# Transposing the copied rows instead of a second product of the second mixing: a transformer layer with a router, one core

## The chip, the core and the metric

The kernel runs on one core of a Trainium2 chip. Time is device time in microseconds (us) of one launch; the median of several launches is compared. TensorE is PE in the profile (PEld for its weight loads), VectorE DVE, ScalarE ACT, GpSimd POOL, and the queue that issues most DMAs SP.

## What is computed

128 sequences of 32 tokens with 256 channels (4096 tokens). `x = x + attention(mix1(x))`, then `x = x + experts(mix2(x))`. A mixing multiplies each sequence by a 32 x 32 matrix of its own; the change touches how the second one is done and how its result reaches the router.

```python
w = weights[conditions]                          # one 32 x 32 matrix per sequence
h = jnp.einsum('bct,bcd->bdt', x, w)             # the second mixing
...
scores = jnp.einsum('btd,de->bte', h, router_w)  # 16 experts
probs = jax.nn.softmax(scores, axis=-1)
routing_weights, routing_idx = jax.lax.top_k(probs, K)      # K = 2
...
out = jnp.einsum('ebtd,bte->btd', expert_out, combine)
```

## The kernel before

The tokens are 32 tiles of 128 rows, in 8 groups (`g`) of 4 tiles. A first phase takes every group through first mixing, quantised projections, attention, output projection, second mixing, router and placement: each row of the second mixing is scattered to DRAM (`routed`) at a place in the list of each of its two experts. A second phase goes through 79 tiles of those lists, a third adds the two results per token and writes the output. The change lies in the first phase alone.

The first phase is a software pipeline written out by hand: each engine has an `iteration(it)` that lists its steps, and runs it for `it` = 0 to 11 (below: **pass** 0 to 11). In pass `it` four groups are in work: `it` (first mixing, projections: PE L1104, L1113, L1137, L1142, L1174), `it - 1` (scores L1189 and L1193, soft maximum, `attend` for tiles 0 and 1), `it - 2` (`attend` L1221 for tiles 2 and 3, output projection L1232), `it - 3` (second mixing and router) and `it - 4` (scatter, POOL L502). So pass 8 is the first with no new group, pass 9 has no scores, and pass 10 has group 7's second mixing alone. Each engine takes its list strictly in order, and engines meet through semaphores.

The second mixing of a group is computed twice on TensorE. `mix2_T` (L1257) gives it transposed, channels on partitions, into the banks `ps_h` (`ps_h[0]` is bank `ps_c`, `ps_h[1]` is `ps_a`): 8 products of 128 columns for two tiles at a time. ScalarE copies it to `hT` (`copy_hT`, L686), from which `router` (L1270) takes its operand. `mix2` (L1244) gives the same numbers by rows into `ps_a`, and ScalarE copies them to `hrow` twice, once for each of a token's experts (`copy_h`, L678). An f32 product shows as two records in the trace, a transpose as one.

What follows the router on VectorE: `rivals` (L917, L919: the two largest scores), `route` (L926 to L932, ends in `both`), then in this order `largest_o` (L845), `row_max` of the second score tile (L880), `factor_o` (L851, L853), `scale_k` (L870), `choose` and `place` (L939 to L962), `row_max` of the third tile, `scale_k`, `step_o` (L860), `norm_o` (L889, L891) and `row_max` of the fourth. `factor_o` lets ScalarE's `round_o` (L593) and with it TensorE's transpose L1127 go; `scale_k` lets TensorE's second `project_k` (L1142) go; each `row_max` lets POOL's `sub_max` (L491) go. On POOL the first two tiles' scatters of a group (four L502) follow the fourth `sub_max` of the pass before. TensorE's `rank` (L1283 to L1286) waits for `both` and for `copy_h`, since it writes `ps_a`. On the SP queue `load_bd2` brings the 32 x 32 matrices of a later group, after `hT_ready` and `h_ready` of the group two before it.

The order of the steps on TensorE from the second mixing on:

```python
mix1(it, 0); mix2_T(it - 3, 0); mix1(it, 1)
attend(it - 2, 2); transpose_p(it - 2, 3); mix2_T(it - 3, 1); attend(it - 2, 3)
mix2(it - 3, 0); scores(it - 1, 0); router(it - 3); scores(it - 1, 1)
mix2(it - 3, 1); scores(it - 1, 2); transpose_x(it, 0); transpose_x(it, 1); spread_s(it)
```

## Time and profile before

| | |
|---|---|
| median of 3 runs | 494.92 us (494.81 to 497.31) |
| the profiled execution | 493.43 us, its span 491.7 us |
| first phase | to about 297 us of the span |
| TensorE busy, whole span | 341.8 us (70%) |
| VectorE / ScalarE / POOL busy | 261.6 / 245.1 / 236.3 us |
| mean granted TensorE clock | 0.876 |
| ScalarE: L678, L686 | 32 of 601 ns, 16 of 595 ns |

Times of a row are from the start of the span. "idle before" is the time for which the engine stood still before that row, and the arrow names who ended it. Matmuls overlap, so the length of a piece of TensorE's work is best taken from the start of its row to the start of the next row.

### The profile page before, as it was taken

The page shows a single profiled execution, that of the slowest core. Times are in us where ns is not written, and L with a number is a line of the kernel's source. Part 1 is how long each engine was busy: PE and PEld are TensorE (multiplying, and loading weights), DVE is VectorE, ACT ScalarE, POOL GpSimd, SP SyncE. Part 2 cuts the span into 40 slices and gives each one's busy share as a digit, 9 for nine tenths or more (in the row PEclk, how much of TensorE's full clock was granted, in tenths as well). Part 3 has the DMA queues.
Part 4 walks back from the last instruction along what each step waited for, and adds up shares of the span by engine and source line. Part 5 has one row for each costly group of instructions (what it writes and reads, how often), then busy time and mean ns, then how long its engine had stood idle before and what let it go on. Part 6 is the DMA issues. An engine that isn't in the chain of part 4 may idle for free.

```text
span 491.7 us, 11060 instructions
## 1 busy us (share of the span) xinstructions
PE 341.8 (70%) x3257; PEld 255.5 (52%) x3257; DVE 261.6 (53%) x913; ACT 245.1 (50%) x580; POOL 236.3 (48%) x248
## 2 busy tenths in 40 slices
PE   0456989989989897958755407988789888981000
PEld 0342647666756566645544306777677767760000
DVE  1635587978869797955744462333233423331531
ACT  9152778866869585845642303454444444440000
POOL 3651231246445555463556361555455555555672
PEclk9977999998999999998965657999899989997555
DMA  6506465365362715353557265544354434413994
GB/s 218 142 3 158 64 154 135 57 131 135 78 185 50 206 44 146 80 144 72 142 147 204 92 245 141 157 128 142 108 149 140 149 119 137 143 33 144 326 381 173
DMA packets 76897, 68.87 MB, mean 140 GB/s; under 512 B 41003, under 2 KB 65968, under 8 KB 76721
## 3 DMA queue, kind: packets, MB, share of 16 engines
q1 hardware_dynamic: 65200, 44.03, 36.0%
q0 software_dynamic: 7296, 20.02, 11.2%
q10 hardware_dynamic: 4352, 4.20, 2.5%
q8 instruction: 28, 0.46, 0.4%
q14 instruction: 21, 0.16, 0.1%
HBM read 35.36 MB, written 30.62 MB: 134 GB/s over the span
## 4 chain that ended last, share of the span: by engine, by line
PE 45%; DVE 17%; issue 9%; DMA 6%; another core or an unknown queue 5%; POOL 5%; ACT 5%; DVEq 4%; SPq 1%; POOLq 0%; ACTq 0%
PE bank L1355 12%; PE bank L1366 7%; DMA arena<-y_d 4%; PE bank L1348 3%; PE bank L1193 3%; PE bank L1244 2%; PE bank L1270 2%; PE bank L1221 2%; PE bank L1127 2%; PE bank L1142 2%; POOL arena L549 2%; DVE stats L898 2%; PE bank L1232 2%; DVE amax L851 2%
## 5 line engine op out<-in xcount | busy, mean ns | idle before, releaser
L542 POOL DMA_INDIRECT y_d<-cen,di x79 | 77.8, 985 | 77.7 <-ACT cen L748 54.0
L1057 DVE SCALAR_TENSOR_TENSOR kT<-kT,hrow,bank 128x96 f32<-128x96 f32 x79 | 24.8, 314 | 98.4 <-ACT kT L743 72.9
L502 POOL DMA_INDIRECT routed<-hrow,posi x64 | 62.8, 982 | 26.7 <-issue 16.8
L1355 PE MATMUL bank<-arena,qT 128*128 x316 | 68.6, 341 | 7.3 <-ACT qT L738 7.3
L491 POOL TENSOR_TENSOR sc<-sc,mx 128x512 f32<-128x512 f32 x32 | 33.6, 1051 | 82.1 <-DVE mx L880 82.0
L1355 PEld LDWEIGHTS bank<-arena,qT 128*128 128x128 f32 x316 | 51.4, 196 | 11.7 <-issue 11.6
L748 ACT ACTIVATE cen<-bank 128x256 f32<-128x256 f32 x79 | 30.6, 387 | 44.7 <-PE bank L1366 33.2
L1366 PE MATMUL bank<-arena,sc 96*128 x158 | 51.3, 408 | 2.0 <-issue 1.0
L1348 PE MATMUL bank<-ident,hrow 128*128 128x128 f32 x158 | 31.9, 285 | 24.5 <-DMA hrow<-routed 19.4
L738 ACT ACTIVATE qT<-bank 128x256 f32<-128x256 f32 x79 | 30.5, 386 | 22.9 <-PE bank L1348 22.7
L1348 PEld LDWEIGHTS bank<-ident,hrow 128*128 128x128 f32 x158 | 23.0, 148 | 33.8 <-DMA hrow<-routed 19.8
L669 ACT ACTIVATE pT<-bank 128x512 f32<-128x512 f32 x32 | 19.7, 614 | 34.5 <-remote 23.3
L1193 PE MATMUL bank<-arena,qT 128*32 128x256 f32 x512 | 36.1, 401 | 0.0
L1221 PE MATMUL bank<-vx,pT 128*32 128x68 f32 x1024 | 23.1, 233 | 16.4 <-ACT pT L669 6.7
L743 ACT ACTIVATE kT<-bank 128x96 f32<-128x96 f32 x79 | 19.9, 252 | 28.3 <-PE bank L1355 21.4
L1221 PEld LDWEIGHTS bank<-vx,pT 128*32 128x32 f32 x1024 | 17.9, 114 | 25.0 <-ACT pT L669 12.8
L549 POOL TENSOR_TENSOR arena<-arena 128x512 f32<-128x512 f32 x16 | 22.2, 1394 | 14.4 <-DMA arena<-y_d 14.3
L1366 PEld LDWEIGHTS bank<-arena,sc 96*128 96x128 f32 x158 | 24.2, 193 | 9.3 <-issue 5.8
L1072 DVE TENSOR_TENSOR X<-X,arena 128x512 f32 (+1 forms) x16 | 14.0, 890 | 27.5 <-POOL arena L549 27.5
L647 ACT ACTIVATE sc<-bank 128x512 f32<-128x512 f32 x32 | 19.4, 605 | 11.6 <-PE bank L1193 11.6
L880 DVE TENSOR_REDUCE mx<-sc 128x16 f32<-128x512 f32 x32 | 21.8, 680 | 6.4 <-ACT sc L647 6.4
L1361 PE MATMUL bank<-ident,kT 128*96 128x128 f32 x79 | 22.2, 281 | 3.3 <-DVE di L1059 3.2
(169 smaller groups left out, 752.9 us busy)
## 6 DMA issues: line engine op xcount, KB each, us to landing
hrow<-routed SPq DMA_DIRECT2D x79, 129.0 KB
arena<-y_d SPq DMA_DIRECT2D x16, 512.0 KB, 5.4
v_d<-v_sb SPq DMA_DIRECT2D x8, 544.0 KB
vx<-v_d SPq DMA_DIRECT2D x32, 136.0 KB
X<-in_x SPq DMA_DIRECT2D x8, 512.0 KB
arena<-kT SPq DMA_DIRECT2D x64, 64.0 KB
out_x<-X ACTq DMA_DIRECT2D x16, 256.0 KB, 5.5
arena<-in_L_ffn_gate_w SPq DMA_DIRECT2D x4, 384.0 KB
```

What stands on the lines that cost most here:

```text
L491: g_.tensor_tensor(sc[t % 2][:, :, :], sc[t % 2][:, :, :], mx[t % 2][:, :].unsqueeze(2).to_broadcast([P, H, SEQ]), ALU.subtract).then_inc( ...
L502: g_.indirect_dma_start(routed, bass.IndirectOffsetOnAxis(ap=posi[g % 2][:, t, k:k + 1], axis=0), hrow[:, g % 2, t, k, :], None).then_inc( ...
L542: g_.indirect_dma_start(y_d, bass.IndirectOffsetOnAxis(ap=di[:, n:n + 1], axis=0), ye[n], None, bounds_check=Y_ROWS - 1, oob_is_err=False) ...
L549: g_.tensor_tensor(fin[j][:, :, 0, :], fin[j][:, :, 0, :], fin[j][:, :, 1, :], ALU.add).then_inc(pair_ok, 1)
L738: a_.activation(xeT[j % 2], bank[j % 2][:, 0:D].rearrange("p (c t) -> p c t", c=KC), ACT.Copy).then_inc(xeT_copied, 1)
L748: a_.activation(ye[n], bank[6 + n % 2][:, 0:D], ACT.Copy).then_inc(ye_copied, 1)
L1057: v.scalar_tensor_tensor(out=hh[n % 2], in0=sg[n % 2], scalar=xe[n][:, D + 1:D + 2], in1=bank[2 + n % 2][:, F:2 * F], op0=ALU.mult, op1=AL ...
L1193: last = t_.matmul(ps_s[t % 2][b * SEQ:(b + 1) * SEQ, c * HC * SEQ:(c + 1) * HC * SEQ], qT[g % 2][:, c, cols], kx[g % 2][:, c, :, cols], s ...
L1221: last = t_.matmul(o[b * SEQ:(b + 1) * SEQ, :, c, :], pT[t % 2][:, c, b * SEQ:(b + 1) * SEQ], vx[:, t * BT + b, :, c * VW:(c + 1) * VW], s ...
L1348: last = t_.transpose(bank[j % 2][:, c * P:(c + 1) * P], xe[j][:, c * P:(c + 1) * P], ident[:, :])
L1355: last = t_.matmul(bank[2 + n][:, 0:2 * F], xeT[n][:, c, :], gu[:, c, bass.ds(expert[m + LAG - 1], 1), :].rearrange("p o f -> p (o f)"), s ...
L1366: t_.matmul(bank[6 + n][:, 0:D], hhT[n], dw[:, bass.ds(expert[m], 1), :].rearrange("p o d -> p (o d)"), start=True, stop=True).then_inc(ye ...
```

## The change

`mix2_T` goes. `mix2` takes its two places and writes `ps_h`; ScalarE copies the rows to `hrow` there, and a new step, `transpose_h`, transposes the copied rows (8 transposes a group in two steps of 4) into `ps_h` for `copy_hT`. The router stands two steps later on TensorE, behind `scores(it - 1, 2)`. Waits follow: `load_bd2` waits for `h_ready` alone, `spread_s` and `rank` for `hT_copied` instead of `h_copied`.

```diff
 load_bd2 (SP):
-                wait(sp, hT_ready, g, 2, 2, lag=2)
                 wait(sp, h_ready, g, 2, 2, lag=2)
 copy_h (ACT):
-                    last = a_.activation(hrow[:, g % 2, 2 * n:2 * n + 2, k, 0:D], ps_a[:, :].rearrange("p (t d) -> p t d", t=2), ACT.Copy)
+                    last = a_.activation(hrow[:, g % 2, 2 * n:2 * n + 2, k, 0:D], ps_h[n][:, :].rearrange("p (t d) -> p t d", t=2), ACT.Copy)
 iteration (ACT):
-                copy_hT(it - 3, 0)
+                copy_h(it - 3, 0)
                 copy_pT(it - 2, 3)
-                copy_hT(it - 3, 1)
+                copy_h(it - 3, 1)
                 centre(it, 0)
                 centre(it, 1)
...
-                copy_h(it - 3, 0)
                 copy_scores(it - 1, 0)
+                copy_hT(it - 3, 0)
+                copy_scores(it - 1, 1)
+                copy_hT(it - 3, 1)
                 centre_o(it - 2)
-                copy_scores(it - 1, 1)
-                copy_h(it - 3, 1)
 spread_s, rank (PE):
-                wait(pe, h_copied, g, 2, 2, lag=3)
+                wait(pe, hT_copied, g, 2, 2, lag=3)
...
-                wait(pe, h_copied, g, 2, 2)
+                wait(pe, hT_copied, g, 2, 2)
 mix2 (PE), which has mix2_T's waits now, and the new step:
+                    last = t_.matmul(ps_h[n][:, k * D:(k + 1) * D], bd2[g % 2][:, t, :, :].rearrange("p b d -> p (b d)"),
+                                     X[:, g * TG + t, :], start=True, stop=True)
+                last.then_inc(h_ready, 1)
+
+            def transpose_h(g, n):
+                if absent(g):
+                    return
+                wait(pe, h_copied, g, 2, n + 1)
+                for c in range(KC):
+                    for k in range(2):
+                        last = t_.transpose(ps_h[n][:, (c * 2 + k) * P:(c * 2 + k + 1) * P], hrow[:, g % 2, 2 * n + k, 0, c * P:(c + 1) * P], ident[:, :])
                 last.then_inc(hT_ready, 1)
 iteration (PE):
-                mix2_T(it - 3, 0)
+                mix2(it - 3, 0)
...
-                mix2_T(it - 3, 1)
+                mix2(it - 3, 1)
                 attend(it - 2, 3)
-                mix2(it - 3, 0)
                 scores(it - 1, 0)
-                router(it - 3)
+                transpose_h(it - 3, 0)
                 scores(it - 1, 1)
-                mix2(it - 3, 1)
+                transpose_h(it - 3, 1)
                 scores(it - 1, 2)
+                router(it - 3)
```

How TensorE's list moves in a pass, from the last `attend` (L1221) to the transpose of a new group (L1113). Before:

```order
L1221 MATMUL bank<-vx,pT 32x4x17 x16
L1244 MATMUL bank<-X,bd_0 128x256 x2
L1189 MATMUL bank<-causal_b,ident_b 128x512
L1193 MATMUL bank<-arena,qT 32x256 x8
L1270 MATMUL bank<-rw,hT 128x16 x8
L1189 MATMUL bank<-causal_b,ident_b 128x512
L1193 MATMUL bank<-arena,qT 32x256 x8
L1244 MATMUL bank<-X,bd_0 128x256 x2
L1189 MATMUL bank<-causal_b,ident_b 128x512
L1193 MATMUL bank<-arena,qT 32x256 x8
L1113 MATMUL bank<-ident,cen 128x128 x8
```

The same piece of the changed kernel, whose lines are numbered anew (L1220 is `attend`, L1188 and L1192 the scores, L1252 `transpose_h`, L1263 the router):

```order
L1220 MATMUL bank<-vx,pT 32x4x17 x16
L1188 MATMUL bank<-causal_b,ident_b 128x512
L1192 MATMUL bank<-arena,qT 32x256 x8
L1252 MATMUL bank<-ident,hrow 128x128 x4
L1188 MATMUL bank<-causal_b,ident_b 128x512
L1192 MATMUL bank<-arena,qT 32x256 x8
L1252 MATMUL bank<-ident,hrow 128x128 x4
L1188 MATMUL bank<-causal_b,ident_b 128x512
L1192 MATMUL bank<-arena,qT 32x256 x8
L1263 MATMUL bank<-rw,hT 128x16 x8
L1112 MATMUL bank<-ident,cen 128x128 x8
```

The two pieces of `mix2` have left this stretch, two pieces of 4 transposes have come, and the router runs behind the third pair of score rows instead of the first.

ScalarE's list from the exponential of the fourth score tile (L658) to the copy of the new group (L602), before:

```order
L658 ACTIVATE pr<-sc,s_qk 128x4x4x32
L686 ACTIVATE hT<-bank 128x2x256
L669 ACTIVATE pT<-bank 128x512
L686 ACTIVATE hT<-bank 128x2x256
L575 ACTIVATE cen<-bank,nmean 128x256 x4
L678 ACTIVATE hrow<-bank 128x2x256 x2
L647 ACTIVATE sc<-bank 128x512
L584 ACTIVATE cen<-cen,nmean 128x256 x4
L647 ACTIVATE sc<-bank 128x512
L678 ACTIVATE hrow<-bank 128x2x256 x2
L602 ACTIVATE xq<-bank 128x512 x2
```

And in the changed kernel (all lines one lower):

```order
L657 ACTIVATE pr<-sc,s_qk 128x4x4x32
L677 ACTIVATE hrow<-bank 128x2x256 x2
L668 ACTIVATE pT<-bank 128x512
L677 ACTIVATE hrow<-bank 128x2x256 x2
L574 ACTIVATE cen<-bank,nmean 128x256 x4
L646 ACTIVATE sc<-bank 128x512
L685 ACTIVATE hT<-bank 128x2x256
L646 ACTIVATE sc<-bank 128x512
L685 ACTIVATE hT<-bank 128x2x256
L583 ACTIVATE cen<-cen,nmean 128x256 x4
L601 ACTIVATE xq<-bank 128x512 x2
```

The double copies to `hrow` have moved ahead of `centre` (L575), and the copies to `hT` behind it, with `centre_o` (L584) after both. VectorE's and POOL's lists are unchanged.

## Rows read from the trace of the kernel before

**Rows 1.** The page: the chain that ended last, by engine

```profile
PE 45%; DVE 17%; issue 9%; DMA 6%; another core or an unknown queue 5%; POOL 5%; ACT 5%; DVEq 4%; SPq 1%; POOLq 0%; ACTq 0%
```

**Rows 2.** Stretches of passes 7, 8: us; busy PE, PEld, DVE, ACT, POOL; PEclk, DMA

```profile
186.50:213.30 26.80, 23.54 (x314) 16.57 (x312) 22.07 (x77) 19.45 (x42) 13.86 (x14) 1.00 0.42 107
213.30:241.20 27.90, 19.62 (x276) 13.72 (x276) 16.26 (x55) 14.65 (x30) 12.98 (x13) 0.88 0.50 122
```

**Rows 3.** Timeline: POOL's scatters and VectorE's wait; start us, length us, engine

```profile
213.44 0.99 POOL L502 DMA_INDIRECT routed<-hrow,posi  x1 [0.15 <-issue]
...
220.67 0.26 DVE L889 RECIPROCAL rs<-bank 128x16 f32<-128x16 f32 x1 [4.90 <-remote]
```

**Rows 4.** Timeline, TensorE, pass 7: a first piece of `mix2_T`

```profile
186.49 1.05 PE L1257 MATMUL bank<-bd,X 128*128 128x128 f32 x8
187.38 0.81 PE L1104 MATMUL bank<-X,bd 128*128 128x256 f32 x3
```

**Rows 5.** Timeline, TensorE, pass 7: from `mix2` to `transpose_x` and beyond

```profile
193.78 1.13 PE L1244 MATMUL bank<-X,bd 128*128 128x256 f32 x4
194.74 0.38 PE L1189 MATMUL bank<-causal_b,ident_b 128*128 128x512 bf16 x1
...
196.05 1.96 PE L1270 MATMUL bank<-rw,hT 128*128 128x16 f32 x16
197.86 0.38 PE L1189 MATMUL bank<-causal_b,ident_b 128*128 128x512 bf16 x1
...
201.45 1.09 PE L1113 MATMUL bank<-ident,cen 128*128 128x128 f32 x8
202.38 1.06 PE L1137 MATMUL bank<-ident,step_of 128*128 128x128 f32 x8
```

**Rows 6.** Timeline, all engines, pass 7: behind the router

```profile
200.26 0.42 DVE L917 MAX8 top<-bank 128x8 f32<-128x16 f32 x4
200.43 1.04 POOL L491 TENSOR_TENSOR sc<-sc,mx 128x512 f32<-128x512 f32 x1 [3.01 <-DVE mx L880]
...
200.75 0.75 DVE L919 TENSOR_TENSOR second<-top 128x4 f32<-128x4 f32 x1
...
201.44 1.04 POOL L485 TENSOR_TENSOR rstd<-veps,half 128x4 f32<-128x4 f32 x1
...
207.15 0.59 PE L1142 MATMUL bank<-xq,wT 128*128 128x512 bf16 x2 [0.43 <-DVE kT L870]
```

**Rows 7.** L917, all its instances: what its engine waited for (us, times)

```profile
  PE bank L1270: 8.9, 3
```

**Rows 8.** Timeline, all engines, pass 8: router, VectorE behind it, POOL

```profile
223.82 2.08 PE L1244 MATMUL bank<-X,bd 128*128 128x256 f32 x4
...
227.16 1.96 PE L1270 MATMUL bank<-rw,hT 128*128 128x16 f32 x16
...
229.16 0.42 DVE L917 MAX8 top<-bank 128x8 f32<-128x16 f32 x4 [0.54 <-PE bank L1270]
232.16 0.68 DVE L880 TENSOR_REDUCE mx<-sc 128x16 f32<-128x512 f32 x1
...
232.93 1.47 DVE L851 TENSOR_SCALAR amax<-amax 128x4 f32<-128x4 f32 x1
...
233.30 1.06 POOL L491 TENSOR_TENSOR sc<-sc,mx 128x512 f32<-128x512 f32 x1
```

**Rows 9.** Timeline, pass 4: `mix2`, router, VectorE behind it

```profile
111.58 1.99 PE L1244 MATMUL bank<-X,bd 128*128 128x256 f32 x4
...
114.72 1.96 PE L1270 MATMUL bank<-rw,hT 128*128 128x16 f32 x16
...
117.80 0.41 DVE L917 MAX8 top<-bank 128x8 f32<-128x16 f32 x4
```

**Rows 10.** Timeline, pass 10 (group 7 alone): `rivals` and `rank`

```profile
274.57 0.42 DVE L917 MAX8 top<-bank 128x8 f32<-128x16 f32 x4 [6.56 <-PE bank L1270]
...
277.69 0.24 PE L1283 MATMUL bank<-both,ones_b 128*128 128x48 bf16 x3 [1.27 <-ACT hrow L678]
```

More of the change, by code:

```diff
@@ L1238, in mix2 @@
                 if n == 0:
-                    wait(pe, hT_copied, g, 2, 2)
-                else:
-                    wait(pe, h_copied, g, 2, 1)
-                for k in range(2):
-                    t = 2 * n + k
-                    last = t_.matmul(ps_a[:, k * D:(k + 1) * D], bd2[g % 2][:, t, :, :].rearrange("p b d -> p (b d)"),
-                                     X[:, g * TG + t, :], start=True, stop=True)
-                last.then_inc(h_ready, 1)
-            def mix2_T(g, n):
-                if absent(g):
-                    return
-                if n == 0:
                     pe.wait_ge(bd2_in[g % 2], 16 * BT * (g // 2 + 1))
@@ L1255, in mix2_T @@
                     t = 2 * n + k
-                    for c in range(KC):
-                        last = t_.matmul(ps_h[n][:, (c * 2 + k) * P:(c * 2 + k + 1) * P],
-                                         X[:, g * TG + t, c * P:(c + 1) * P],
-                                         bd2[g % 2][:, t, :, :].rearrange("p b d -> p (b d)"), start=True, stop=True)
+                    last = t_.matmul(ps_h[n][:, k * D:(k + 1) * D], bd2[g % 2][:, t, :, :].rearrange("p b d -> p (b d)"),
[8 more added lines that the diff above has]
+                        last = t_.transpose(ps_h[n][:, (c * 2 + k) * P:(c * 2 + k + 1) * P], hrow[:, g % 2, 2 * n + k, 0, c * P:(c + 1) * P], ident[:, :])
                 last.then_inc(hT_ready, 1)
@@ L1296, in iteration @@
                 transpose_p(it - 2, 3)
-                mix2_T(it - 3, 1)
+                mix2(it - 3, 1)
                 attend(it - 2, 3)
-                mix2(it - 3, 0)
                 scores(it - 1, 0)
+                transpose_h(it - 3, 0)
+                scores(it - 1, 1)
+                transpose_h(it - 3, 1)
+                scores(it - 1, 2)
                 router(it - 3)
-                scores(it - 1, 1)
-                mix2(it - 3, 1)
-                scores(it - 1, 2)
                 transpose_x(it, 0)
```

## The prediction

> **What bounds the kernel now.** I read the chain of work that ended last, then busy time by pass, then the timeline of single passes, then what each step waited for. The chain gives TensorE the largest share, 45% [rows 1]; but most of that lies in the expert phase, which the change leaves alone, and the chain says nothing of who holds a pass of the first phase. The busy times do: in pass 7, a full one, TensorE works 23.5 of 26.8 us and VectorE 22.1 [rows 2]. Both are nearly full, so their order against each other decides.
>
> A pass has three parts. First a stall: POOL issues scatters back to back, and VectorE, which waits for an `attend`, gets its release only near their end. In pass 8 the scatters begin at 213.44, six of them some 1.3 us apart, and VectorE starts at 220.67 after 4.90 us idle [rows 3]. I do not know why TensorE's completions come so late there; what matters is that the scatters start behind the last `sub_max` of the pass before, which hangs on VectorE's last `row_max`. Second, from that release on, VectorE works through its list with hardly a gap, up to `factor_o` and `scale_k`, and TensorE waits for it: the second `project_k` stood 0.43 us for `scale_k` [rows 6]. Third, TensorE's work behind that. VectorE's list thus runs the whole pass, and it contains `rivals`, which needs the router. In three of eight groups VectorE stood idle for the router, 8.9 us in all [rows 7]; in the other five the router had long been done.
>
> **What the change takes and adds on TensorE.** A piece of `mix2_T` costs 0.89 us from its start to the next row's [rows 4], two pieces 1.78 us a group. `mix2` stays: 0.96 us a piece [rows 5], now in the places of `mix2_T`, so the stretch before the stall grows by 2 x 0.07 = 0.14 us, inside the stall. Added are 8 transposes; 8 of the same shape take 0.93 us [rows 5]. Net 1.78 - 0.93 = 0.85 us a group, 6.8 us over 8 groups. If TensorE set every pass, that would be the gain. All of it falls between the last `attend` and `transpose_x`, where VectorE is what the rest waits for, so I count it at nothing: `transpose_x` and its copy come 0.8 us earlier, and TensorE then waits that much longer for `scale_k`.
>
> **What it moves.** The router now ends later. Before, from `mix2` on: 0.96 (mix2) + 1.31 (scores) + 1.81 (router) = 4.08 us. Now: 3 x 1.31 + 0.93 + 1.81 = 6.67 us [rows 5]. So the router ends 2.6 us later, counted from the same release. What that does depends on the pass:
>
> Pass 7. The router ended at 196.05 + 1.96 = 198.01, VectorE came to `rivals` at 200.26 [rows 5, 6]. Now 200.6: `rivals` starts 0.4 us late. But L919 behind it ended with POOL's L491, at 201.50 against 201.47 [rows 6]; started 0.4 us later it ends at the same moment. Cost 0, bounds 0 and 0.4. Passes 3, 5 and 6 have the same sequence and were not among the waiting ones [rows 7]: 0 each, bounds the same.
>
> Pass 4. TensorE is slow at its start: the first `mix2` took 3.14 - 1.31 = 1.83 us until the scores instead of 0.96, and the router ended at 116.68 with `rivals` at 117.80, a slack of 1.1 us instead of 2.3 [rows 9]. The first scores now fall into the slow stretch; I take 2.2 us for them (between 1.31 and twice that), which keeps the shift at 2.6. `rivals` is 1.5 us late. Of this the wait of L919 swallows up to 0.6 (0.75 us long in rows 6) and the one at L851 some more. I take 0.6 us; bounds 0 and 1.5.
>
> Pass 8. No new group, so VectorE is free early and `rivals` starts 0.04 us after the router's end at 229.12 [rows 8]. Here 2.6 us come through. Behind it L851 waits for POOL's L491, which itself started at 233.30, 0.46 us after `row_max` ended at 232.84, since POOL was busy [rows 8]; with VectorE later, that 0.46 goes. Cost 2.2 us; bounds 1.2 (the whole 1.47 us of L851 swallowed) and 2.6. The loss goes on through `row_max`, `sub_max` and the scatters into pass 9, by the chain of rows 3. That the first `row_max` comes earlier, since scores no longer follow `mix2`, helps nobody: `rivals` is next in VectorE's list.
>
> Passes 9 and 10 have no scores. Counted from the second piece of the second mixing, the router waited for one copy to `hT` (0.6 us) and a `mix2` (0.96). Now it waits for the double copy to `hrow` (1.2), four transposes (0.47) and a copy to `hT` (0.6), 0.7 us more. In pass 10 this is met by a wait that goes: `rank` stood 1.27 us for the last `copy_h`, which was done long after `rivals` [rows 10], and now that copy precedes the router. I take 0 for pass 9 (bounds 0 and 0.7) and -0.2 for pass 10 (bounds -0.6 and 0.4).
>
> The rest I cost at nothing, with its cover. ScalarE has 1.2 instead of 0.6 us before `centre`, and `centre` was waiting on VectorE's variance anyway. The copies to `hT` are done before the router's turn as long as the third scores (1.31) run between. `load_bd2` is no longer held by the second `mix2` and goes out some us earlier on SP, past nothing but a wait; its matrices are needed a pass later. `spread_s` and `rank` wait for copies made before.
>
> **The sum**, against the profiled execution of 493.43 us: 0 + 0.6 + 2.2 + 0 - 0.2 = +2.6, so 496.0. The median of the runs shown is 494.92, 1.5 above it; I state the forecast against the median: **497.5 us**. The ends of the bounds add to +0.6 and +6.8, that is 495.5 and 501.7. A measurement here tells 0.5%, about 2.5 us, from no change.
>
> **A rule against the change.** L919 and L851 end when POOL's instruction ends [rows 6, 8]. The Trainium skill, page "SBUF — State Buffer", section "Who interferes with whom", says that the two engines share one port pair as an exclusive lock, and that a tensor_tensor with two SBUF inputs, or a VectorE op in a two-port mode, is blocked for the whole of a GpSimd instruction that holds it. By that rule L919, once it starts after 201.47 instead of before, is caught by the next holder too.
>
> **The rivals.**
> 1. *L919 meets the next POOL instruction.* If the router ends some 0.4 us later than I worked out, L919 starts behind L491 and lies under L485, which ran from 201.44 to 202.48 [rows 6]: 1.0 us in passes 3, 5, 6 and 7, or at least 0.4 without a block. For it: the margin is a few tenths. Against it: L919 must come that late in each pass. Time 497.5 + 4 x 0.4 to 4 x 1.0, 499.1 to 501.5, say 500.0. Chance 0.18.
> 2. *TensorE sets the passes* (the other side). Then VectorE's wait for the router is no price and the 0.85 us a group come back: 494.92 - 6.8 = 488.1. For it: TensorE has 23.5 us of work in 26.8 [rows 2]. It decides from the point where TensorE's waits for VectorE in a pass (0.43 us for `scale_k`) are shorter than the time that VectorE can be pulled forward; against it, VectorE's list has no wait for TensorE in that part that becomes shorter. Chance 0.13.
> 3. *The late router costs nothing visible.* Pass 8 ends by the scatters and their DMAs rather than by VectorE, or passes 4 and 8 swallow most: +0.4, 495.3. For it: the stall's length is unexplained [rows 3]. Chance 0.20.
> 4. The forecast, 496.3 to 499.0: chance 0.49.
>
> Faster by over 0.5%: rival 2 and a little, 0.14. Slower by over 0.5% (above 497.4): rival 1 and somewhat over half of the forecast's case, 0.18 + 0.30 = 0.48. Within: 0.38. The range leaves out rival 2 and the far end of rival 1: 493.5 to 501.0.
>
> **What would show it.** Right: in passes 5 to 7 the length from one stall to the next stays at about 27 us, with TensorE idle before the second `project_k` longer by some 0.8 us; in pass 8 `rivals` starts within 0.1 us of the router's end and TensorE's transposes of the third part (L1127) stand idle over 2 us; `rank` in pass 10 no longer waits for `copy_h`. L919 ends with L491. Wrong: passes 5 to 7 shorter by 0.8 us (rival 2), L919 longer than 1 us or starting behind L491 (rival 1), pass 8 no longer than before (rival 3).

## The result and the profile after

| | before | changed |
|---|---|---|
| median, runs side by side | 497.23 us (20 runs, 492.40 to 503.54) | 501.30 us (20 runs, 498.45 to 505.08) |
| ratio, 95% interval | | 1.0093 [1.0067, 1.0118] |
| profiled execution, its span | 493.43 us, 491.7 | 499.03 us, 497.3 |
| TensorE / VectorE busy | 341.8 / 261.6 us | 336.7 / 257.5 us |
| last scatter of the first phase starts | 291.0 us | 292.9 us |

The change makes the kernel slower, by 0.9% (4.1 us between the medians, 4.6 by the ratio), although TensorE is busy for 5.1 us less. The kernel before itself came out 2.3 us above the 494.92 us of its first three runs, so the ratio says more of the change than the time does; the forecast as a ratio was 497.5 / 494.92 = 1.0052. The two profiled executions differ by 5.6 us, but not all of that is the change. From the last scatter to the end, where the code is the same, four profiles (two of each kernel) took 200.7, 204.8 (before), 204.4 and 202.8 us (changed): no difference that stands out of their spread. The same four put the last scatter at 291.0 and 288.6 (before) and at 292.9 and 294.6 us (changed): 4.0 us in the mean, against up to 2.4 us between two profiles of one kernel. So most of the loss, as far as four profiles can tell, lies in the first phase, and its passes are compared from here on.

The page of the changed kernel: the chain by engine, which answers to [rows 1], and the granted clock in slices of some 12.4 us.

```profile
PE 48%; DVE 16%; issue 9%; DMA 7%; another core or an unknown queue 5%; POOL 4%; ACT 4%; DVEq 4%; SPq 1%; POOLq 0%; ACTq 0%
...
PEclk9968999999999999977765757999899989987555
```

Passes 7 and 8 from first scatter to first scatter, the view of [rows 2].

```profile
184.80:212.35 27.55, 23.57 (x307) 15.77 (x306) 21.59 (x78) 19.57 (x43) 14.10 (x14) 1.00 0.42 102
212.35:243.05 30.70, 20.99 (x266) 13.87 (x266) 15.83 (x55) 14.23 (x29) 12.98 (x14) 0.72 0.53 135
```

Between the same marks (186.3, 213.4, 241.4 us) the kernel before had 27.2 and 28.0 us. A full pass stays nearly as long as it was. Pass 8 is 2.7 us longer, and its mean granted clock is 0.72 where it was 0.88.

**A full pass.** The timeline of pass 7, TensorE, VectorE and POOL behind the last `attend`, answers to [rows 5, 6]. `mix2` is L1242 now, `transpose_h` L1252, the router L1263, `rivals` L916 and L918.

```profile
193.95 0.66 PE L1252 MATMUL bank<-ident,hrow 128*128 128x128 f32 x4
...
197.92 1.96 PE L1263 MATMUL bank<-rw,hT 128*128 128x16 f32 x16 [0.30 <-ACT hT L685]
199.27 1.05 POOL L490 TENSOR_TENSOR sc<-sc,mx 128x512 f32<-128x512 f32 x1 [3.00 <-DVE mx L879]
...
199.92 0.42 DVE L916 MAX8 top<-bank 128x8 f32<-128x16 f32 x4 [0.74 <-PE bank L1263]
200.28 1.04 POOL L484 TENSOR_TENSOR rstd<-veps,half 128x4 f32<-128x4 f32 x1
200.42 0.17 DVE L918 TENSOR_TENSOR second<-top 128x4 f32<-128x4 f32 x1
...
203.95 1.04 POOL L490 TENSOR_TENSOR sc<-sc,mx 128x512 f32<-128x512 f32 x1
203.96 1.06 DVE L850 TENSOR_SCALAR amax<-amax 128x4 f32<-128x4 f32 x1
...
206.06 0.59 PE L1141 MATMUL bank<-xq,wT 128*128 128x512 bf16 x2 [1.08 <-DVE kT L869]
```

The router ended at 199.88, and VectorE stood 0.74 us for it. But L918, which before lay 0.75 us under POOL's subtraction and ended with it, now takes 0.17 us. The 0.74 us of new wait and the 0.58 us of old blocking trade places.

**The ledger of VectorE** in the whole execution, from the groups of instructions by line. First the kernel before:

```profile
L851 DVE TENSOR_SCALAR amax<-amax 128x4 f32<-128x4 f32 x8 | 10.9, 1365 | 0.7
L919 DVE TENSOR_TENSOR second<-top 128x4 f32<-128x4 f32 x8 | 4.2, 528 | 0.6
L917 DVE MAX8 top<-bank 128x8 f32<-128x16 f32 x32 | 3.3, 166 | 8.9 <-PE bank L1270 8.9
```

and the changed one:

```profile
L850 DVE TENSOR_SCALAR amax<-amax 128x4 f32<-128x4 f32 x8 | 8.9, 1112 | 0.7
...
L916 DVE MAX8 top<-bank 128x8 f32<-128x16 f32 x32 | 3.4, 169 | 16.6 <-PE bank L1263 16.5
...
L918 DVE TENSOR_TENSOR second<-top 128x4 f32<-128x4 f32 x8 | 1.8, 230 | 0.6
```

The wait for the router grew from 8.9 us in 3 groups to 16.5 in 7 [rows 7], by 7.6. The two instructions that POOL blocks became 2.0 and 2.4 us shorter. That leaves 3.2 us. Between the second profiles of the two kernels the same sums are 9.5 us of new wait and 0.4 and 2.4 us of shorter blocking, which leaves 6.7. The first phase became 2.0 us longer between the first profiles and 6.0 between the second, so the ledger gives the direction and the order of size, not the figure.

**Pass 8**, the answer to [rows 8]:

```profile
228.88 1.96 PE L1263 MATMUL bank<-rw,hT 128*128 128x16 f32 x16
...
231.09 0.43 DVE L916 MAX8 top<-bank 128x8 f32<-128x16 f32 x4 [4.35 <-PE bank L1263]
...
234.85 1.04 POOL L490 TENSOR_TENSOR sc<-sc,mx 128x512 f32<-128x512 f32 x1 [3.49 <-DVE mx L879]
234.86 1.06 DVE L850 TENSOR_SCALAR amax<-amax 128x4 f32<-128x4 f32 x1
...
237.96 1.97 PE L1126 MATMUL bank<-ident,cen 128*128 128x128 f32 x8 [1.23 <-ACT cen L592]
```

VectorE stands 4.35 us for the router here, 0.54 before. The chain of waits for this stretch passes from the router to VectorE and on to TensorE's transposes; the columns are start, length, what.

```profile
228.95 2.12 PE bank L1263 x16
...
232.96 1.22 DVE amax L844
...
234.86 1.06 DVE amax L850
...
236.62 1.30 ACT cen L592 x3
...
237.96 1.97 PE bank L1126 x8
```

TensorE's clock adds to it. While VectorE works off what it could not do earlier, TensorE waits, and the next stretch runs at the lower of the two clock levels (0.50 in the table by stretches; 1.2 GHz):

```profile
231.80:242.00 10.20, 7.67 (x76) 5.47 (x77) 8.80 (x29) 6.11 (x13) 2.25 (x3) 0.50 0.51 129
```

The 8 transposes L1126 take 1.97 us in it; 8 such transposes at the full clock took 1.07 in pass 7 (0.93 to the next row in [rows 5]). Before, the pass had one slow stretch, at 219.2 to 226.0 us, from the end of the stall on. How much the clock takes varies: the second profile of the changed kernel has its long slow stretch at the stall (218.8 to 229.1 us) and only a short one behind (235.9 to 239.3), and its L1126 ran at the full clock (1.09 us). In all, TensorE is at the lower level for 17.1 and 13.6 us of pass 8 in the changed kernel, and for 6.8 us in both profiles of the kernel before.

### The profile page after: what moved, and what is told of

Same layout as the page of the kernel before. It is cut to its first block, busy times and chain, and to the rows that moved or that the text cites. A ratio compares the mean times of both kernels' runs of the same rounds, so it can differ in the third digit from the quotient of the medians.

```text
span 497.3 us, 10926 instructions
## 1 busy us (share of the span) xinstructions
PE 336.7 (68%) x3193; PEld 247.3 (50%) x3193; DVE 257.5 (52%) x913; ACT 244.4 (49%) x580; POOL 236.4 (48%) x248
## 4 chain that ended last, share of the span: by engine, by line
PE 48%; DVE 16%; issue 9%; DMA 7%; another core or an unknown queue 5%; POOL 4%; ACT 4%; DVEq 4%; SPq 1%; POOLq 0%; ACTq 0%
PE bank L1348 13%; PE bank L1359 7%; PE bank L1192 5%; DMA arena<-y_d 4%; PE bank L1263 3%; PE bank L1341 3%; PE bank L1220 2%; PE bank L1126 2%; DVE amax L850 2%; PE bank L1141 2%; PE bank L1354 2%; PE bank L1231 2%; PE bank L1252 2%; DVE stats L791 2%
## 5 line engine op out<-in xcount | busy, mean ns | idle before, releaser
L1056 DVE SCALAR_TENSOR_TENSOR kT<-kT,hrow,bank 128x96 f32<-128x96 f32 x79 | 24.8, 314 | 102.5 <-ACT kT L742 83.0
L1348 PE MATMUL bank<-arena,qT 128*128 x316 | 69.9, 346 | 5.9 <-ACT qT L737 5.6
L490 POOL TENSOR_TENSOR sc<-sc,mx 128x512 f32<-128x512 f32 x32 | 33.6, 1050 | 82.9 <-DVE mx L879 82.7
L1348 PEld LDWEIGHTS bank<-arena,qT 128*128 128x128 f32 x316 | 52.8, 201 | 10.4 <-issue 10.1
L747 ACT ACTIVATE cen<-bank 128x256 f32<-128x256 f32 x79 | 30.6, 387 | 44.4 <-PE bank L1359 27.9
L1341 PE MATMUL bank<-ident,hrow 128*128 128x128 f32 x158 | 32.2, 287 | 24.5 <-DMA hrow<-routed 19.6
L737 ACT ACTIVATE qT<-bank 128x256 f32<-128x256 f32 x79 | 30.5, 386 | 24.8 <-PE bank L1341 22.9
L1220 PE MATMUL bank<-vx,pT 128*32 128x68 f32 x1024 | 23.2, 233 | 23.3 <-DVE cen L890 22.4
L1192 PE MATMUL bank<-arena,qT 128*32 128x256 f32 x512 | 37.0, 410 | 0.0
L668 ACT ACTIVATE pT<-bank 128x512 f32<-128x512 f32 x32 | 19.5, 610 | 32.5 <-remote 27.7
L1220 PEld LDWEIGHTS bank<-vx,pT 128*32 128x32 f32 x1024 | 18.0, 114 | 34.5 <-ACT pT L668 27.0
L742 ACT ACTIVATE kT<-bank 128x96 f32<-128x96 f32 x79 | 20.0, 253 | 30.7 <-PE bank L1348 24.7
L1071 DVE TENSOR_TENSOR X<-X,arena 128x512 f32 (+1 forms) x16 | 14.0, 890 | 27.8 <-POOL arena L548 27.8
```

The costliest lines, as they stand in the source:

```text
L490: g_.tensor_tensor(sc[t % 2][:, :, :], sc[t % 2][:, :, :], mx[t % 2][:, :].unsqueeze(2).to_broadcast([P, H, SEQ]), ALU.subtract).then_inc( ...
L737: a_.activation(xeT[j % 2], bank[j % 2][:, 0:D].rearrange("p (c t) -> p c t", c=KC), ACT.Copy).then_inc(xeT_copied, 1)
L747: a_.activation(ye[n], bank[6 + n % 2][:, 0:D], ACT.Copy).then_inc(ye_copied, 1)
L1056: v.scalar_tensor_tensor(out=hh[n % 2], in0=sg[n % 2], scalar=xe[n][:, D + 1:D + 2], in1=bank[2 + n % 2][:, F:2 * F], op0=ALU.mult, op1=AL ...
L1192: last = t_.matmul(ps_s[t % 2][b * SEQ:(b + 1) * SEQ, c * HC * SEQ:(c + 1) * HC * SEQ], qT[g % 2][:, c, cols], kx[g % 2][:, c, :, cols], s ...
L1220: last = t_.matmul(o[b * SEQ:(b + 1) * SEQ, :, c, :], pT[t % 2][:, c, b * SEQ:(b + 1) * SEQ], vx[:, t * BT + b, :, c * VW:(c + 1) * VW], s ...
```

## The experiments

Ratios are to the kernel before, run beside each kernel on the same chip, with 95% intervals. The runs were made on several chips: the controls, "router earlier" and "router's place alone" on one where the kernel before took 494.24 us; "router earlier from pass 8 on", "`rivals` later, changed" and the first two with moved scatters on a second (500.51 us); the rest on a third (501.24 us). On the second and third chip the changed kernel itself was not run, so a comparison with its 1.0093 and 1.0133 is one across sets of runs, and so is one of profiles. In the table "rivals" is the time in pass 8 from VectorE's release (L889, L888) to `rivals`, "stall" that from pass 8's first scatter to the release.

| run | ratio | full passes 4 to 7 | pass 8: stall, rivals, whole | passes 9 + 10 | last scatter |
|---|---|---|---|---|---|
| before, 1st profile | 1 | 27.9 27.6 27.2 27.2 | 7.2, 8.5, 28.0 | 38.5 | 291.0 |
| before again | | 27.3 27.6 27.2 27.2 | 8.6, 8.4, 29.1 | 36.1 | 288.6 |
| changed | 1.0093 [1.0067, 1.0118] | 27.3 27.4 27.2 27.6 | 8.8, 10.0, 30.7 | 38.8 | 292.9 |
| changed again | 1.0133 [1.0078, 1.0188] | 27.9 27.6 27.2 27.4 | 8.8, 11.2, 31.8 | 38.4 | 294.6 |
| router earlier | 1.0073 [1.0038, 1.0107] | 27.2 27.7 27.2 26.9 | 8.8, 9.6, 30.2 | 38.5 | 292.4 |
| router's place alone | 1.0252 [1.0181, 1.0323] | 27.6 27.7 27.6 27.8 | 8.7, 11.9, 32.5 | 41.3 | 300.0 |
| router earlier from pass 8 on | 1.0041 [1.0002, 1.0080] | 28.0 27.6 27.3 27.5 | 8.9, 9.0, 32.1 | 37.7 | 295.8 |
| `rivals` later, changed | 1.0011 [0.9984, 1.0038] | 27.3 26.9 27.1 27.6 | 8.9, 10.5, 30.1 | 39.9 | 292.4 |
| `rivals` later, before | 0.9999 [0.9964, 1.0034] | 26.8 26.8 26.3 27.8 | 8.8, 11.0, 30.0 | 39.3 | 290.9 |
| the dropped wait put back | 1.0033 [0.9997, 1.0070] | 27.3 27.6 27.3 27.4 | 8.8, 11.1, 31.7 | 38.1 | 293.0 |

**Controls.** Both kernels again, unchanged.

> The changed kernel once more, to see what of the +5.6 us between the two profiles is fixed. In them the first phase was 1.9 us longer (last scatter at 292.9 instead of 291.0 us) and the expert phase, whose code is the same, 3.7 us. If the late router is the whole cause (theory A), the time is 2 to 3 us over the kernel before, and the expert phase of this profile lies between the two. If the change also slows the expert phase (theory B), it is 4 to 6 us over, and the expert phase is again about 3.5 us longer than before.

> The kernel before once more, for a second profile. Theory A: last scatter near 291 us, expert phase anywhere within some 3 us of the first profile's 200.7. Theory B: expert phase within 1 us of 200.7.

The changed kernel: 499.55 us, ratio 1.0133 [1.0078, 1.0188]; before, one profiled execution, 495.18 us. The direction and the pattern by pass come again. The second profile of before shows what the first did not: the stall of pass 8 varies without any change, 7.2 and 8.6 us.

**Router's place alone.** This tells the place of the router from the rest of the change: `mix2_T` and both copies stay as before, only the router moves behind the third scores.

```diff
                 scores(it - 1, 0)
-                router(it - 3)
                 scores(it - 1, 1)
                 mix2(it - 3, 1)
                 scores(it - 1, 2)
+                router(it - 3)
```

> The kernel before with the router alone moved behind scores(it - 1, 2); mix2_T and mix2 stay. Theory A: pass 8 longer by the 2.6 us of two score pieces less what VectorE gives back, 2 to 3.5 us slower than before (the mix2 piece is now ahead of the router too, up to +1 us more), pass 10 and 9 up to 1 us slower each. Rival (the loss comes from transposes and copies): no change within 1 us.

Measured 508.15 us, 1.0252 [1.0181, 1.0323]: worse than the whole change. Here two pieces of `mix2` lie in front of the router where the change has transposes, and VectorE's wait for it (the groups by line) is

```profile
L917 DVE MAX8 top<-bank 128x8 f32<-128x16 f32 x32 | 3.4, 170 | 23.7 <-PE bank L1270 23.7
L919 DVE TENSOR_TENSOR second<-top 128x4 f32<-128x4 f32 x8 | 1.3, 166 | 0.6
```

The wait is 14.8 us longer than before, and L919 never blocked. The late place of the router is thus enough for a loss, and for a much larger one than the 2 to 3.5 us that were expected (and up to 1 more in each of passes 9 and 10). Against the mean of the two profiles of before, pass 8 is 4.0 us longer, passes 9 and 10 together 4.0, and the full passes, 27.6 to 27.8 us, 1.1 us in sum: what they can absorb is used up.

**Router earlier in the changed kernel**, with the scores moved behind it, in all passes and then from pass 8 on alone (the condition is `it >= GROUPS`). ScalarE's copies are put in the same order each time; that part of the edits is left out here.

```diff
 iteration (PE), all passes:
-                scores(it - 1, 0)
                 transpose_h(it - 3, 0)
-                scores(it - 1, 1)
+                scores(it - 1, 0)
                 transpose_h(it - 3, 1)
-                scores(it - 1, 2)
+                scores(it - 1, 1)
                 router(it - 3)
+                scores(it - 1, 2)
 iteration (PE), from pass 8 on:
-                scores(it - 1, 1)
-                transpose_h(it - 3, 1)
+                if it >= GROUPS:
+                    transpose_h(it - 3, 1)
+                    router(it - 3)
+                    scores(it - 1, 1)
+                else:
+                    scores(it - 1, 1)
+                    transpose_h(it - 3, 1)
                 scores(it - 1, 2)
-                router(it - 3)
+                if it < GROUPS:
+                    router(it - 3)
```

> The changed kernel with its router (and both transposes) two steps earlier, behind scores(it - 1, 1) instead of scores(it - 1, 2). Theory A (late router costs pass 8 some 2.7 us, through VectorE's list in order): the router ends about 1.3 us earlier in every pass, pass 8 is 1.3 us shorter, 1 to 2 us faster than the changed kernel. Rival (TensorE's transposes and ScalarE's copies are the cost, wherever the router stands): same time as the changed kernel.

> The changed kernel, with the router (and the second piece of transposes) earlier in passes 8 to 10 alone, behind the first scores; passes 3 to 7 as in the change. Before, VectorE came to rivals in pass 8 8.4 us after its release from the stall, in the changed kernel 10.0 and 11.2 us. If that wait is what the change costs (theory A), it comes back to 8.5 to 9.5 us, pass 8 is 1 to 2 us shorter than in the changed kernel, and the whole 1 to 2.5 us faster than it. Rival (the full passes, or the stalls' own length, make the loss): same as the changed kernel within 1 us.

The results are 1.0073 [1.0038, 1.0107] and 1.0041 [1.0002, 1.0080]. The first, 497.99 us, is 1.6 us below the changed kernel beside it (499.55), the 1 to 2 us expected, but the intervals overlap (the changed kernel's starts at 1.0078), so it doesn't settle the matter. Its pass 8 is 30.2 us long, 0.5 and 1.6 us less than in the two profiles of the changed kernel, where 1.3 were expected. The timeline shows why the router gains little there:

```profile
223.30 1.12 PE L1252 MATMUL bank<-ident,hrow 128*128 128x128 f32 x4
...
224.45 0.60 ACT L685 ACTIVATE hT<-bank 128x512 f32<-128x512 f32 x1 [1.49 <-PE bank L1252]
226.64 1.12 PE L1252 MATMUL bank<-ident,hrow 128*128 128x128 f32 x4
227.79 0.60 ACT L685 ACTIVATE hT<-bank 128x512 f32<-128x512 f32 x1 [0.42 <-PE bank L1252]
228.98 1.96 PE L1263 MATMUL bank<-rw,hT 128*128 128x16 f32 x16
```

The router starts at 228.98, no earlier than the 228.88 of the changed kernel: behind the stall TensorE is at half clock (221.0 to 227.8 us), 4 transposes take 1.12 us, and the second piece comes only behind the scores. In the second variant the time from release to `rivals` does fall, to 9.0 us, but pass 8 is 32.1 us long: ScalarE now stands 4.04 us for the second scores behind the router, and VectorE 2.26 us for ScalarE's `centre_o` behind their copy. In pass 8 an earlier router is bought with later scores. The ratio of this variant is the lower one all the same, with the last scatter at 295.8 us in its profile: a single profile and the ratio do not agree here, and I rest nothing on that run but the shape of pass 8.

**`rivals` later on VectorE.** Instead of the router, its waiter is moved, in the changed kernel and, as a control, in the kernel before.

```diff
 iteration (DVE):
-                rivals(it - 3)
-                route(it - 3)
                 largest_o(it - 2)
                 row_max(it - 1, 1)
+                rivals(it - 3)
+                route(it - 3)
```

> The changed kernel, with VectorE's rivals and route behind largest_o and the second row_max (1.9 us of its own work) instead of ahead of them; router where the change puts it. Theory A (VectorE, in order, stands for the router in pass 8): the wait before L916 shrinks from 3 to 4 us to 1 to 2 us, the time to factor_o falls by up to 1.9 us in pass 8 and stays in the full passes: 1.5 to 2.5 us faster than the changed kernel. Rival (VectorE's wait is not on the path; TensorE or the stall sets pass 8): no change.

> The kernel before with VectorE's list reordered alone: the rivals and route of group it-3 go behind largest_o and row_max(it-1,1), as in the run that did the same to the changed kernel (ratio 1.0011 there, where the change alone had 1.0133 and 1.0093). Theory A, the loss is a late router that VectorE waits for, and the reorder gives VectorE other work in that wait: here the router's sums are there in time in the full passes, so there is little to win, and the rivals come some 1.8 us later for nothing but are taken up further down; ratio 0.997 to 1.003, last scatter within 1.5 us of the 288.6 and 291.0 us of the two profiles of before. Theory B, the new order is simply better for any router: ratio 0.990 to 0.995, about the 4 to 6 us that it gave with the change in.

The changed kernel comes back to 1.0011 [0.9984, 1.0038]; the kernel before stays at 0.9999 [0.9964, 1.0034]. So the new order is not better by itself. Where the router is early it is worth nothing; where it is late, 0.8 to 1.2% by the ratios, if the changed kernel has on this chip the ratio that it has elsewhere. The groups by line of the changed kernel with it:

```profile
L844 DVE TENSOR_REDUCE amax<-cen 128x4 f32<-128x1024 f32 x8 | 9.7, 1218 | 6.4 <-ACT cen L583 6.4
L850 DVE TENSOR_SCALAR amax<-amax 128x4 f32<-128x4 f32 x8 | 5.1, 643 | 0.8
L916 DVE MAX8 top<-bank 128x8 f32<-128x16 f32 x32 | 3.4, 170 | 9.3 <-PE bank L1263 9.3
L918 DVE TENSOR_TENSOR second<-top 128x4 f32<-128x4 f32 x8 | 2.7, 343 | 0.9 <-issue 0.4
```

The wait for the router is down from 16.5 to 9.3 us. This was meant as the test of the forecast's cause: fill VectorE's wait for the router with other work, and the loss should be gone, though the router, the transposes and the copies are all where the change put them. By the ratio it is gone. The trace supports it in pass 8, where `factor_o` ends 13.3 us after the release (13.7 and 13.5 before, 14.8 and 16.1 changed), but the test is less clean than its ratio. Most of the wait was not filled: VectorE now stands 6.4 us for ScalarE's `centre_o` (L844), 3.25 of them in pass 8, where it stood 0.0 us in the kernel before and in the changed one. The two waits together are 15.7 us, 0.8 less than the 16.5 of the changed kernel; what fell more are the instructions that POOL blocks, L850 and L918, by 2.9 us. And in this profile the first phase is not shorter, with the last scatter at 292.4 us and 39.9 us for passes 9 and 10. So the run agrees with a late router as the cause and doesn't prove it; the run with the router's place alone is the stronger evidence. What can be said of the 5.1 us that TensorE saves is that they bring nothing here either.

**The dropped wait put back.** SyncE's load of the matrices waits for `hT_ready` again.

```diff
 load_bd2 (SP):
+                wait(sp, hT_ready, g, 2, 2, lag=2)
                 wait(sp, h_ready, g, 2, 2, lag=2)
```

> The changed kernel with the one wait put back that it dropped on SyncE: the load of the second mixing's weights also waits for the transposed rows to be copied. Theory A, passes 9 and 10 (about 1.3 us longer than before in sum, where 0.2 less was forecast) are longer because the router is late there too and TensorE's list is short: the wait changes nothing, ratio 1.005 to 1.013, last scatter 292 to 295. Theory B, the weights that now start some 5 us earlier collide with the scatters or with the first expert's weights and lengthen the hold-up of pass 9 (8.7 instead of 5.7 us in one profile of three): the hold-up is 5.7 us, and the ratio 1.000 to 1.005.

1.0033 [0.9997, 1.0070], with the last scatter at 293.0 us and pass 9's stall at 7.2. The ratio fits the second theory and the trace the first (292 to 295 us); neither stall (5.7) nor last scatter moved as the second asked. The interval touches that of the changed kernel (from 1.0067). This is inconclusive: the earlier load may cost nothing or a good part of the loss. The run is a warning besides. It differs from the changed kernel by one wait and has 1.0033 on the third chip, as "router earlier from pass 8 on" has 1.0041 on the second. The changed kernel may lose less on these chips than on the first, and then less than 0.8% was there for the later `rivals` to mend. Only a run of the changed kernel on these chips would tell, and there is none.

**The stall, and scatters elsewhere.** The prediction left unexplained why TensorE's completions come late at the start of a pass. Moving the scatters tests whether they are the cause: behind `rstd_x` on POOL, in the kernel before and in the changed one.

```diff
 iteration (POOL):
+                rstd_x(it)
                 scatter(it - 4, 0)
                 scatter(it - 4, 1)
-                rstd_x(it)
...
-                scatter(it - 4, 2)
...
                 sub_max(it - 1, 0)
                 rstd_o(it - 2)
-                scatter(it - 4, 3)
+                scatter(it - 4, 2)
                 sub_max(it - 1, 1)
+                scatter(it - 4, 3)
```

> The kernel before, with POOL's four scatters at the start of a pass moved behind rstd_x, where POOL stood idle, and the next two behind it. In both profiles VectorE and ScalarE get TensorE's completions only 6.0 us after the first scatter in every full pass and 7 to 9 us in passes 8 and 9. If the scatters hold them back (theory S), that wait goes to about 0.5 us past the attend, each full pass is some 2.5 to 3 us shorter, passes 8 and 9 4 to 6 us: 15 to 20 us faster. Rival (the copies of k or v by DMA, or TensorE itself, hold them): the stall stays where it is, no change within 2 us; a third way: the stall moves with the scatters and costs the same there.

> The same move of the scatters in the changed kernel. Theory S: as much faster against the changed kernel as the other one against the kernel before; and with the stall gone the two differ by what the late router costs VectorE alone. If TensorE becomes the bound of the full passes then (0.85 us a group less work in the changed kernel), the changed kernel comes out up to 4 us ahead of its counterpart; if VectorE stays the bound, 2 to 4 us behind.

The kernel before: 486.31 us, 0.9713 [0.9671, 0.9755], 14 us faster where 15 to 20 were expected. The changed kernel: 503.41 us, 1.0019 [0.9972, 1.0066], no gain on the kernel before, where as much was expected as in it. In the kernel before passes 4 to 6 fall to 25.2, 25.4 and 25.1 us, TensorE busy for all but 0.6 us of the last of them (stretch of one pass, columns as in [rows 2]):

```profile
160.00:185.10 25.10, 24.51 (x318) 17.50 (x316) 22.33 (x78) 19.76 (x43) 14.10 (x15) 1.00 0.50 124
```

VectorE's waits before L889 that end with "remote", the profile's word for a releaser that it can't name, fall from 17.8 us to 7.0. But the late completions are not gone; they fall wherever the scatters go. In the timeline of the changed kernel they fall on the very chain that the change has built, and the same three passes take 29.0 to 29.4 us:

```profile
167.55 1.04 POOL L501 DMA_INDIRECT routed<-hrow,posi  x1 [0.20 <-issue]
...
169.57 0.66 PE L1252 MATMUL bank<-ident,hrow 128*128 128x128 f32 x4
...
173.39 0.60 ACT L646 ACTIVATE sc<-bank 128x512 f32<-128x512 f32 x1 [3.15 <-remote]
173.88 0.59 ACT L685 ACTIVATE hT<-bank 128x512 f32<-128x512 f32 x1
...
174.53 3.59 PE L1263 MATMUL bank<-rw,hT 128*128 128x16 f32 x16 [2.77 <-ACT hT L685]
...
178.16 0.43 DVE L916 MAX8 top<-bank 128x8 f32<-128x16 f32 x4 [5.09 <-PE bank L1263]
```

The second scores and the transposes are done on TensorE by about 170.3 us, but ScalarE sees them at 173.39, some 5.8 us after the first scatter. Only then come the copy to `hT` and the router, and that at half clock (granted clock 0.50; 3.59 us instead of 1.96). VectorE's wait for the router adds up to 34.0 us. In the kernel before with the same move, the router's operand is copied before the scatters start (L686 at 157.74, first scatter at 159.88), and the delay falls on the second scores: ScalarE stands 1.77 us for them and VectorE only 0.33 us before `rivals`.

**Scatters still later in the changed kernel**: behind `sub_max` 0 and `rstd_o`, then one tile each behind `sub_max` 1 and 2.

```diff
 iteration (POOL):
-                scatter(it - 4, 0)
-                scatter(it - 4, 1)
                 rstd_x(it)
...
-                scatter(it - 4, 2)
...
                 sub_max(it - 1, 0)
                 rstd_o(it - 2)
+                scatter(it - 4, 0)
+                scatter(it - 4, 1)
...
+                sub_max(it - 1, 1)
+                scatter(it - 4, 2)
+                sub_max(it - 1, 2)
                 scatter(it - 4, 3)
-                sub_max(it - 1, 1)
-                sub_max(it - 1, 2)
                 sub_max(it - 1, 3)
```

> The changed kernel with POOL's scatters still further back: behind sub_max(it-1,0) and rstd_o, two of them, then one tile's behind sub_max 1 and one behind sub_max 2. Theory A, the scatters hold back the completions of TensorE that fall into the 6 us from their start, and moving them behind rstd_x made the hold-up fall on scores(1), the transposes of the copied rows and the router: with the first one at about the router's own end those steps are free, the full passes fall from 27.3 to 25 to 26 us, last scatter 280 to 286, ratio to before 0.975 to 0.990. Theory B, wherever the scatters stand in the changed kernel the hold-up finds a chain that is waited for (here scores(2) to sub_max(2) and the mixing of the next pass): full passes stay at 27 us or over, ratio 1.005 or more.

487.83 us, 0.9773 [0.9714, 0.9833], last scatter 281.3: within the first theory's numbers for the ratio and the scatter, but not for the reason it gave. The full passes stay at 27.3 to 27.7 us, as the second theory had it. The gain of 11.6 us in the last scatter, against the first profile of the changed kernel, is all in the passes without a new group, where the stall had been longest: from L1126 to L1126 passes 8 and 9 take 25.1 and 18.4 us, where they took 30.8 and 27.1. "Remote" is no longer named before L888; it stands before other steps (L953 in pass 10 for 2.4 us, and in the full passes `oq`, as in this timeline row):

```profile
181.43 1.08 ACT L608 ACTIVATE oq<-bank 128x512 bf16<-128x512 f32 x2 [1.91 <-remote]
```

**Both on the kernel before**: scatters behind `rstd_x` and `rivals` behind `row_max`, the edits shown above together.

> The kernel before with both: scatters behind rstd_x (ratio 0.9713 alone) and rivals behind row_max(1). Theory A, with the scatters behind rstd_x the router falls into their hold-up also in the kernel before, and VectorE's wait for it is filled by the reorder: 1 to 4 us more than alone, ratio 0.963 to 0.970. Theory B, the router of the kernel before stands early enough, the reorder only makes the positions later: ratio 0.971 to 0.976, passes of 25.1 to 25.4 us as alone.

483.51 us, 0.9672 [0.9612, 0.9732], passes of 25.2, 24.8 and 24.5 us. It is the fastest kernel of the study and beats both kernels, but its interval overlaps that of the scatters alone (0.9671 to 0.9755, on another chip), so the reorder's share is not settled.

## Why the prediction was right and wrong

The direction and the mechanism held, the size did not: 1.0093 against 1.0052, and 501.3 us lies 0.3 above the range. Three things made up the miss. The forecast was stated from a median of three runs, and the kernel before came out 2.3 us higher beside the changed one; applied to the old median, the measured ratio would give 499.5 us, inside the range. The sum of +2.6 us was short of the 4.0 us of the first phase (means of two profiles each): passes 9 and 10 fell 1.5 us short and pass 8 0.5, and pass 4 gave 0.6 back. And the range ended at 501.0, below the 501.7 of the prediction's own bounds.

- **Full passes 5 to 7, forecast 0 each.** Right, and by the route given: the router is late in every pass (wait named before L916 in 7 groups of 8), and the shorter blocking by POOL takes it up. Passes 4 to 7 together are 109.9 and 109.4 us before, 109.4 and 110.0 changed. The router's place alone shows the limit: with VectorE's waits 14.8 us longer in sum, each full pass is some 0.3 us longer.
- **Pass 4, forecast +0.6.** Wrong by that much: `rivals` came at 117.81, against 117.80 [rows 9], in a pass that had begun 0.6 us earlier; between the second profiles it came 1.6 us later in the pass. L918 ran in 0.17 us and L850 in 1.28 (1.06 in the second profile), and the mean length of the pass is the same, 27.6 us. I had named both waits and taken too little for them.
- **Pass 8, forecast +2.2.** The release-to-`rivals` time grew by 1.5 and 2.8 us in the two profiles, 2.2 in the mean, and in the rest of the pass 0.3 came back: the mechanism and nearly the size. What the term lacked is that the pass grew by 2.7 us. Its stall was 8.8 us twice, where before had 7.2 and 8.6. I had treated the stall as fixed from one profile; the run with `rivals` later in the kernel before has 8.8, so a long one does not need the change. The longer time at the lower clock was not in the sum either; it may be why only 0.3 us came back, which no run tests.
- **Passes 9 and 10, forecast -0.2: the step that failed.** Together they took 38.5 and 36.1 us before, 38.8 and 38.4 changed: +1.3 in the mean, 0.5 in pass 9 and 0.8 in pass 10. In pass 10 the longer way to the router was priced nearly right: from the copy behind the second piece of the second mixing to the router it is 2.48 us, twice, where it was 1.61, twice, so 0.87 more against a forecast of 0.7. But `rivals` came 1.4 us later in the pass in the mean, since in the second changed profile the router ran at the lower clock (3.10 us; 1.96 in the first); VectorE's wait for it was 6.6 and 6.0 us before, 7.1 and 8.4 changed. And the credit was taken from one profile. From `rivals` to the first scatter of the next pass the kernel before needed 5.3 us there, with `rank` waiting for `copy_h` [rows 10] behind a second `mix2` at the lower clock (2.05 us); in its second profile, where that `mix2` took 1.11 us, it needed 4.1, as both changed profiles do. In pass 9, which the forecast put at 0, the stall lasted 8.6 us in one of the changed profiles and 5.7 in the other three; why stays open, and putting the SyncE wait back did not decide it. All this is less than the 2.4 us by which the two profiles of before differ in these passes.
- **TensorE's saving, counted at nothing.** Right. It was 5.1 us of busy time in sum (7.3 between the second profiles; forecast 6.8), and TensorE's waits for `scale_k` (L1142, now L1141) rose from 1.6 to 5.6 us in exchange (2.1 to 4.5); in pass 7 from 0.43 to 1.08 us, near the 0.8 us that the forecast named. Rival 2 fell by this and by the ratio.
- **Rival 1, L919 meets POOL's next instruction.** It did meet it: L918 at 200.42 lies inside L484, 200.28 to 201.32, and it took 0.17 us. It took no longer in any of the 22 passes, over all runs here, in which it started under that instruction. Started more than 0.1 us before the end of the subtraction of 128x512 it ended with that every time. The Trainium skill, page "SBUF — State Buffer", section "Who interferes with whom", has the loser blocked for the whole instruction. That agrees with L850 under L490 (1.06 us, ending with it), and not with L918 under L484, an operation of 128x4 whose record is as long (1.04 us). What the small instruction holds, and for how long, no run here shows.
- **Rival 3, the late router costs nothing visible**, fell by the ratio, and by pass 8; its argument, that the stall is unexplained, was the best lead to a faster kernel.
- Two signs were wrong. L1126 was to stand idle over 2 us in pass 8; it stood 1.23 and 1.58 us. And L919, now L918, no longer ends with POOL's subtraction in passes 4, 6 and 7, where it was to. A third is undecided: `rivals` was to start within 0.1 us of the router's end in pass 8, and started 0.25 us behind it in one profile and 0.03 in the other.

## What to carry to other kernels

Moving a producer later cost mainly in the passes in which its waiter has nothing else to do; look first at the passes that lack a part of the pipeline's work, and put the waiter behind work that is ready before you give up a cheaper producer. A new wait can be free where it takes the place of another engine's blocking, up to the length of that blocking (0.8 us a pass here, the mean of passes 4 to 7). Before a term is taken from a single profile, see in a second one whether it is there at all. Work taken off an engine that waits for another each pass comes back as a longer wait, so ask what the waiting one would do with the time. And when a stretch in the profile is unexplained, test it by moving what runs beside it: that was worth 14 us here, three times the whole loss looked for.

## What was not expected of the hardware

While GpSimd issues indirect scatters back to back, other engines see TensorE's completions late: 5.8 to 6.4 us after the first scatter in passes 4 to 7 of the kernels with the scatters at the start, 7.2 to 8.9 us in pass 8, where six follow each other. With the scatters behind `rstd_x` the delay moved with them, to steps that were not delayed before. That the scatters bring it about is shown by this move; by what path is not. One candidate is in the profile: the 16 DMA engines are all busy just before the release, in pass 7 of the kernel before from 190.5 to 192.0 us (a share of 1.03 to 1.05 in the view by stretches; release at 192.26), in pass 8 from 219.0 to 220.5 (1.06 to 1.10; release at 220.67), and with the moved scatters of the changed kernel from 171.0 to 173.0 (1.10 to 1.18; ScalarE released at 173.39). SyncE issues large copies at about the same time (`v_sb` to `v_d`, 544 KB, at 188.95 us in pass 7), so the scatters need not be alone in it. No run had fewer or smaller scatters, and none moved those copies.
